# A new order of blocks and PSUM banks in a four-layer graph kernel

## What is computed

```python
x = _layernorm(x + _L0_gnn_ref(x, adj, ...))  # 8 heads: tanh(A * (Xc Xp^T)) Xp, relu
x = _layernorm(x + _L1_gnn_ref(x, adj, ...))  # two hypergraph convolutions, relu and norm between
x = _layernorm(x + _L2_gnn_ref(x, adj, ...))  # H = sum over k of (T^k X) Wk, T from exp(leaky_relu(sj + si)) * A
x = _layernorm(x + _L3_gnn_ref(x, adj, ...))  # gate, sigmoid(xg Wqk^T), scores * A, Wl and Wr
```

## Time and profile before

| | us |
|---|---|
| median of 3 runs | 1873.93 |
| lowest and highest run | 1869.39, 1875.06 |
| the profiled execution | 1869.13 |
| its span in the trace | 1867.3 |
| PE busy in the span | 1799.6 |
| DVE busy | 1657.4 |
| ACT busy | 1236.0 |
| POOL busy | 897.8 |

### The profile page before, as it was taken

How to read it: one execution, slowest core, us unless ns; L and a number is a source line. 1 busy time by engine, 2 the same in 40 slices (tenths; PEclk the granted TensorE clock), 3 DMA queues, 4 the chain that set the end, 5 groups by cost and what they waited for, 6 DMA issues and landing times. The chain is left out here.

```text
span 1867.3 us, 50617 instructions
## 1 busy us (share of the span) xinstructions
PE 1799.6 (96%) x14472; PEld 1569.0 (84%) x14472; DVE 1657.4 (89%) x4508; ACT 1236.0 (66%) x2384; POOL 897.8 (48%) x1743
## 2 busy tenths in 40 slices
PE   5789999999999999999999999999999999999985
PEld 4678888888888888888888888888888888888864
DVE  4779999999999999999999999999999999999874
ACT  4557666676676766766766766766667667676653
POOL 1335445445455455455545544544544545545542
PEclk9999999999999999999999999999999999999998
DMA  4111111211111111211111221111121111121110
GB/s 158 46 30 43 62 38 55 62 47 45 62 51 42 62 51 42 62 53 39 62 59 34 62 62 35 58 62 37 55 62 47 46 62 51 42 62 51 32 36 27
DMA packets 99483, 97.63 MB, mean 52 GB/s; under 512 B 8320, under 2 KB 90368, under 8 KB 99200
## 3 DMA queue, kind: packets, MB, share of 16 engines
q1 hardware_dynamic: 99456, 97.29, 17.0%
HBM read 80.48 MB, written 16.78 MB: 52 GB/s over the span
## 5 line engine op out<-in xcount | busy, mean ns | idle before, releaser
L416 ACT ACTIVATE x<-res,shift,rstd 128x256 f32<-128x256 f32 x512 | 283.4, 614 | 22.7 <-issue 10.4
L316 POOL TENSOR_TENSOR var_eps<-mean_var,eps 128x2 f32<-128x2 f32 x192 | 38.0, 198 | 417.2 <-DVE mean_var L618 417.2
L321 POOL TENSOR_TENSOR rstd<-var_eps,minus_half 128x2 f32<-128x2 f32 x256 | 194.3, 759 | 20.0
L626 DVE TENSOR_TENSOR masked<-psum,adjT 128x512 f32<-128x512 f32 x256 | 169.6, 684 | 23.0 <-PE psum L1035 23.0
L610 DVE BATCH_NORM_STATS2 stats<-res 128x6 f32<-128x256 f32 x512 | 189.5, 412 | 0.3
L969 PE MATMUL psum<-wk_hi,xT_hi 128*128 128x258 f32 (+1 forms) x512 | 186.2, 364 | 3.5 <-DVE res L920 2.1
L404 POOL TENSOR_TENSOR rz<-rz,vec 128x512 f32<-128x512 f32 x64 | 81.5, 1274 | 210.1 <-ACT rz L595 210.1
L969 PE MATMUL psum<-wk_hi,xT_lo 128*128 128x258 f32 (+1 forms) x512 | 173.6, 339 | 0.0
L969 PE MATMUL psum<-wk_lo,xT_hi 128*128 128x258 f32 (+1 forms) x512 | 173.5, 339 | 0.0
L969 PE MATMUL psum<-w_hi,zT_hi 128*128 128x256 f32 x512 | 147.0, 287 | 4.6 <-DVE zT_lo L605 4.6
L969 PE MATMUL psum<-w_hi,zT_lo 128*128 128x256 f32 x512 | 144.4, 282 | 0.0
(11 more groups left out here) (180 smaller groups left out, 6169.9 us busy)
## 6 DMA issues: line engine op xcount, KB each, us to landing
adjT<-in_adj_t SPq DMA_DIRECT2D x256, 128.0 KB, 2.3
xt_in<-in_xt SPq DMA_DIRECT2D x64, 256.0 KB, 2.7
x<-in_x SPq DMA_DIRECT2D x64, 256.0 KB, 2.8
out<-x SPq DMA_DIRECT2D x64, 256.0 KB, 2.2
wts<-in_adj SPq DMA_DIRECT2D x64, 128.0 KB, 2.2
wts<-in_w SPq DMA_DIRECT2D x1, 1028.0 KB, 10.6
wts<-in_w SPq DMA_DIRECT2D x1, 1024.0 KB, 7.3
wts<-in_w SPq DMA_DIRECT2D x1, 769.0 KB, 11.8
```

Source lines behind the costliest of these rows:

```text
L316: pool.tensor_tensor(var_eps[k][:, :], mean_var[k][:, :, 1], (eps_quarter if k == 1 else eps)[:, :], ALU.add)
L321: pool.tensor_tensor(rstd[k][:, :], var_eps[k][:, :], minus_half[:, :], ALU.pow) \
L416: last = act.activation(xs[k + 1][:, g, :], res[k][:, g, :], ACT.Identity, scale=rstd[k][:, g:g + 1], bias=shift[k][:, g:g + 1])
L626: dve.tensor_tensor(masked[:, q, :, :, :], ps(f"att_{q}").rearrange("p (g c n) -> p g c n", g=G, c=NC), adjT[0][:, :, :].unsqueeze(2).to_b ...
```

## The change

No computation is altered. The order of the blocks on all five engines, the banks of the PSUM tenants, and the places where weights are prepared in the first turns are new. Some blocks change the turn in which they run: the load of `xs[0]` and the tanh of heads 2 and 3 from stage 1 at the top to stage 0 at the bottom, `layer_stats(0)` and the reciprocal `att_r` from the bottom of a turn to the top of the next. PE's `claim` now takes several names and merges waits for one signal. The core of the diff:

```diff
 TENANTS = [
-    ("xp", 3, 0, "xp_read"), ("y12_0", 4, 4, "y12_read_0"), ("xpT", 6, 0, "xpT_read"), ("zT_0", 2, 2, "zT_lo_0"),
+    ("xp", 6, 0, "xp_read"), ("y12_0", 5, 4, "y12_read_0"), ("xpT", 4, 0, "xpT_read"), ("zT_0", 6, 2, "zT_lo_0"),
...
-    ("headsT", 1, 0, "headsT_read"), ("y0_0", 7, 3, "y0_read_0"), ("y0_1", 6, 3, "y0_read_1"),
-    ("mix_0", 2, 5, "mix_read_0"), ("heads", 4, 0, "res0"), ("mix_1", 1, 5, "mix_read_1"),
+    ("headsT", 5, 0, "headsT_read"), ("y0_0", 2, 3, "y0_read_0"), ("y0_1", 7, 3, "y0_read_1"),
+    ("mix_0", 0, 5, "mix_read_0"), ("heads", 4, 0, "res0"), ("mix_1", 1, 5, "mix_read_1"),
 ]
...
@@ POOL @@
+                if on[3]:
+                    rstd_of(1, n[3], p[3])
+                if on[6]:
+                    rstd_of(3, n[6], p[6])
                 if on[4]:
                     if t.first(4):
                         pool.wait_ge(sem("bk_bc"), 1)
                     wait(pool, "y0_read_1", n[4])
                     pool.tensor_tensor(y0[:, :, 0:D], y0[:, :, 0:D], rows(bk_bc), ALU.add).then_inc(sem("y0_bias"), 1)
-                if on[3]:
-                    rstd_of(1, n[3], p[3])
-                if on[6]:
-                    rstd_of(3, n[6], p[6])
+                if t.first(2):
+                    pool.wait_ge(sem("wlr_hi"), 1)
+                    pool.tensor_tensor(wlr_lo[:, :, :], wlr_f[:, :, :], value(wlr_hi[:, :, :]), ALU.subtract).then_inc(sem("wlr_lo"), 1)
+                    pool.wait_ge(sem("wk12_hi"), 1)
...
@@ ACT @@
-                if on[1]:
-                    wait(act, "pxT", p[1])
-                    wait(act, "x1_rest", p[1])
-                    normalise(0, n[1])
                 if on[0]:
                     wait(act, "att_3", p[0])
                     wait(act, "xcT", n[0])
                     act.activation(xcT[:, :, :, :].rearrange("p c g n -> p (c g n)"), ps("xcT"), ACT.Copy) \
                         .then_inc(sem("xcT_read"), 1)
...
+                if on[1]:
+                    wait(act, "pxT", p[1])
+                    wait(act, "x1_rest", p[1])
+                    normalise(0, n[1])
...
@@ DVE @@
+                if on[4]:
+                    wait(dve, "hop2_read", p[4])
+                    wait(dve, "hop1_1", n[4])
+                    sums, _ = both("hop1_0", "hop1_1", slice(D, D + 1))
+                    dve.tensor_scalar(row_s[:, :].unsqueeze(2), sums, 1e-12, None, ALU.add).then_inc(sem("rows_0"), 1)
+                if on[1]:
+                    wait(dve, "prop_read", n[1])
+                    dve.tensor_scalar(deg_m[:, :], prop[:, :, P], 1.2e-38, None, ALU.max).then_inc(sem("deg_inv_0"), 1)
+                if on[4]:
+                    wait(dve, "rows_0", n[4])
+                    dve.reciprocal(row_r[:, :], row_s[:, :]).then_inc(sem("rows_1"), 1)
...
@@ PE @@
-                    for q in range(NQ):
-                        claim(f"att_{q}", t)
+                    claim("att_0 att_1 att_2 att_3", t)
```

More of the change, by code:

```diff
@@ L434, in turn @@
                     hi(xT2_hi[:, :, :, :].rearrange("p c g n -> p (c g n)"), ps("xT2"), "xT2_hi")
[L435 to L439, removed]
+                if t.first(0):
+                    act.wait_ge(sem("w_0"), 32)
+                    act.activation(wp_hi[:, :, :], wp_f[:, :, :], ACT.Copy).then_inc(sem("wp_hi"), 1)
                 if on[0]:
@@ L445, in turn @@
                 if on[2]:
+                    wait(act, "z", p[2])
+                    wait(act, "hid_stats", p[2])
+                    wait(act, "hid_read_0", n[2])
+                    act.activation(hid_relu[:, 0, :], hid[:, 0, :], ACT.Relu).then_inc(sem("hid_relu_0"), 1)
                     wait(act, "z", p[2])
@@ L567, in turn @@
                     hi(pxT_hi[:, :, :, :].rearrange("p c g n -> p (c g n)"), ps("pxT"), "pxT_hi")
+                if on[0]:
+                    wait(act, "headsT", p[0])
+                    wait(act, "masked_1", n[0])
+                    act.activation(att[:, 0:2, :, :, :], masked[:, 0:2, :, :, :], ACT.Tanh).then_inc(sem("tanh_0"), 1)
                 if on[5]:
@@ L578, in turn @@
                     normalise(3, n[6])
[L579 to L582, removed]
+                if on[5]:
+                    wait(act, "mix_1", p[5])
+                    wait(act, "mix_read_1", p[5])
+                    wait(act, "rz_0", n[5])
+                    act.activation(rz3[:, 0, 0:2 * D], ps("rz_0"), ACT.Copy).then_inc(sem("rz_read_0"), 1)
                 if on[3]:
@@ L730, in turn @@
                     dve.tensor_tensor(bk_bc[:, :], bk_01[:, :], bk_3[:, 2, :], ALU.add).then_inc(sem("bk_bc"), 1)
-                if on[2]:
-                    if t.first(2):
-                        dve.wait_ge(sem("beta_w2"), 1)
-                    read_y1(0, n[2], p[2])
+                if on[4]:
+                    wait(dve, "hop2", p[4])
+                    wait(dve, "adj2_loaded", n[4], 16)
+                    wait(dve, "e_exp", n[4])
+                    dve.tensor_tensor(alpha[:, :, :], e_exp[:, :, :], adjT[2][:, :, :], ALU.mult) \
+                        .then_inc(sem("alpha"), 1)
+                if on[6]:
+                    layer_stats(3, n[6])
+                if t.first(2):
+                    dve.wait_ge(sem("wqk_hi"), 1)
+                    lo(wqk_lo[:, :, :], wqk_f[:, :, :], value(wqk_hi[:, :, :]), "wqk_lo")
+                if on[3]:
+                    aggregate(1, n[3], p[3])
+                if on[6]:
+                    aggregate(3, n[6], p[6])
                 if t.first(1):
@@ L828, in turn @@
                     last.then_inc(sem("hop2_read"), 1)
+                if t.first(1):
+                    dve.wait_ge(sem("beta_turned"), 1)
+                    dve.tensor_copy(beta_w2[:, :], ps("y1_0")[:, 0:D]).then_inc(sem("beta_w2"), 1)
+                if t.first(0):
+                    dve.wait_ge(sem("w_2"), 32)
+                    for a in range(2):
+                        for c in range(NC):
+                            dve.tensor_tensor(aw_prod[:, a * NC + c, :], wv_f[:, c, :], aw_bc[:, a, :], ALU.mult)
+                        last = dve.tensor_tensor(aw_prod[:, 2 * NC + a, :], bv_bc[:, :], aw_bc[:, a, :], ALU.mult)
+                    last.then_inc(sem("aw_prod"), 1)
+                    dve.wait_ge(sem("aw_prod"), 1)
+                    dve.tensor_reduce(u_col[:, :], aw_prod[:, :, :], AX.X, ALU.add).then_inc(sem("u_col"), 1)
                 if on[1]:
@@ L837, in turn @@
                 if on[0]:
-                    mask(3, n[0], p[0])
+                    wait(dve, "inc", n[0])
+                    dve.tensor_reduce(edge_n[:, :], inc[:, :, :], AX.X, ALU.add).then_inc(sem("edge_n"), 1)
                 if on[4]:
@@ L841, in turn @@
                 if on[0]:
-                    wait(dve, "inc", n[0])
-                    dve.tensor_reduce(edge_n[:, :], inc[:, :, :], AX.X, ALU.add).then_inc(sem("edge_n"), 1)
+                    wait(dve, "edge_n", n[0])
+                    dve.tensor_scalar(edge_m[:, :], edge_n[:, :], 1.0, None, ALU.max).then_inc(sem("edge_0"), 1)
+                if on[4]:
+                    aggregate(2, n[4], p[4])
+                if t.first(0):
+                    dve.wait_ge(sem("w1_hi"), 1)
+                    lo(w1_lo[:, :, :], w1_f[:, :, :], value(w1_hi[:, :, :]), "w1_lo")
                 if on[2]:
@@ L952, in claim @@
                 if not t.static:
-                    at = mates.index(u)
-                    mates = [mates[at - 1]]
+                    mates = [mates[mates.index(u) - 1]]
                 for v in mates:
                     _, _, stage, emptied = TENANTS[v]
-                    wait(pe, emptied, t.n[stage] if v < u else t.p[stage])
+                    yield emptied, t.n[stage] if v < u else t.p[stage]
+            def claim(names, t, *also):
+                found = {}
+                for signal, count in also:
+                    whole, part = part_of(signal)
+                    found[whole, count] = part or 0, signal
+                for name in names.split():
+                    if t.static and BANK[TENANT[name]] in taken:
+                        pe.wait_ge(sem("beta_w2"), 1)
+                    for signal, count in waits_of(name, t):
+                        whole, part = part_of(signal)
+                        found[whole, count] = max(found.get((whole, count), (0, "")), (part or 0, signal))
+                for (_, count), (_, signal) in found.items():
+                    wait(pe, signal, count)
             def claim_once(name, t):
@@ L1009, in y1_of @@
             def y1_of(g, t, n):
-                claim(f"y1_{g}", t)
-                wait(pe, f"zT_lo_{g}", n)
+                claim(f"y1_{g}", t, (f"zT_lo_{g}", n))
                 split_product(ps(f"y1_{g}")[:, 0:D],
@@ L1150, in turn @@
                     rz_of(0, t)
+                if t.first(1):
+                    pe.wait_ge(sem("beta_bc"), 1)
+                    claim_once("y1_0", t)
+                    for k in range(NK):
```

(10 more changed lines are left out.)

255 lines of the change are left out of this document (100 added, 155 removed), and 8 rows, old and new, of the table TENANTS.

## The result

The changed kernel is slower: 1881.48 us, the median of 7 runs (1878.35 to 1889.68), against 1873.93 us before (7 runs, 1869.39 to 1877.48). The ratio is 1.0048, with a 95% interval of 1.003 to 1.0066, so 0.5% and clear of no change. The forecast said 1894, slower by 1.1%.

The account below looks back on a forecast made before the run. PE, busy throughout the steady turns, was taken as the bound. From the profiled 1869.1 us, +26.6 (steady turns) and -3.4 (ramp and drain) gave 1892.3, or 1897.1 from the median; the forecast was 1894, range 1860 to 1905.

Parts of the forecast that it names:

- What bounds the kernel: Steady turns: PE busy throughout 27.76 us, so time freed on DVE or POOL buys nothing; only blocks reaching PE late count.
- deg_m inside y0_bias: Steady turn: deg_m, now before row_r, starts inside POOL's y0_bias and ends with it, 912.65 instead of 912.00, delaying hop1 reads.
- The walk: Following one steady turn's DVE and POOL instructions in the new order: hop2's weight load at 913.87 instead of 913.48.
- 59 x 0.45 = 26.6: Steady loss: PE waits 0.45 us more before hop2 in each of 59 turns, +26.6 us in all.
- I cost this at nothing: PE is busy throughout and hides it: Steady turns: edge_m, xg, e_exp and res3 leaving the port gain nothing, though edge_m alone gives DVE 0.5 us per turn.
- Ramp and drain: Outside the steady turns: waits for res0 and xcT saved, weight preparation and res3 costing; sum -3.4 us, from -6 to +3.
- the weight preparation: Ramp: wlr_lo and wk12_lo together on POOL in turn 2, in front of turn 3's xT0_lo; up to +2.3 us.
- xcT's wait: Ramp and drain: PE waits 4.2 us in three turns for xcT's read; the longest goes, -1.7 us.
- A: Rival, faster: deg_m starts before y0_bias or is spared the port, so hop2 is on time; 1860.4 us; chance 0.28.
- B: Rival, no difference: PE sees nothing of the change, ramp and drain exchange waits; 1869 to 1876 us; chance 0.14.
- C: Rival, slower: x_rest keeps xg off the port, PE's conv waits up to 1.0 us per turn; 1925 us; chance 0.03.
- D: Rival, slower: short POOL instructions also keep DVE out, rstd1's pow delaying inc through qkT 0.3 us; 1884 us; chance 0.03.

Follow-up runs that it names:

- y0_late: The changed kernel with an unused 0.69 us power instruction on POOL in front of y0_bias; 1854.79 us, 0.9886 of the kernel before.
- y0_plus: The changed kernel with an unused 0.20 us multiply on POOL in front of y0_bias; 1890.57 us, 1.0091 of the kernel before.
- deg_back: The changed kernel with only deg_m moved back behind the hop1 reads on DVE; 1855.35 us, 0.9894 of the kernel before.
- before_sj_edge: The kernel before with, on DVE, sj and sj5 in front of the first zT_lo and edge_m directly behind edge_n; 1880.73 us, ratio 1.0036.
- edge_back: deg_back with edge_m and edge_r moved behind deg on DVE, where edge_m stood in the kernel before; 1855.7 us, ratio 0.9902.
- ramp_free: The kernel before with POOL's x1_rest, in turns 2 to 5 only, waiting for the turn's second zT_lo; 1868.58 us, ratio 0.9978.
- best: deg_back with wlr_lo prepared in turn 3 on POOL and, in the drain, PE's xT2 before gram; 1852.49 us, ratio 0.9885.

## Why the prediction was right in place and wrong in size

**What bounds the kernel, right but for one conclusion.** The loss in the steady turns is PE's wait for one block, by tenths of a microsecond in each turn. That time freed on DVE buys nothing there did not follow; this is the step that failed, below.

**deg_m inside y0_bias, right.** The walk had y0_bias 0.40 us ahead of deg_m; it was 0.28. It had hop2's load 0.40 us later; 0.63 against 0.21 is 0.42. The missing 0.12 us of the lead arose mainly where the prediction had feared it: a small instruction of rstd1 met inc and took 0.33 us instead of 0.20, and y0_bias came later by about as much.

```profile
915.33 0.29 DVE L768 TENSOR_SCALAR inc<-adjT 128x256 f32<-128x256 f32 x1
...
915.34 0.33 POOL L315 TENSOR_TENSOR neg_mean<-mean_var,minus_one 128x2 f32<-128x2 f32 x1
```

The rule of the Trainium skill ("SBUF — State Buffer", section "SBUF: two separate sides", an exclusive lock kept by whoever starts first) agrees with y0_late and y0_plus for the long instructions. For a short POOL instruction that starts first it does not hold here: deg_m took 0.15 us inside the power instruction.

**The term of the sum that failed: 59 x 0.45 = 26.6.** Measured are 57 x 0.30 = 17.1 us (1599.57 and 1599.85 against 1582.45 and 1582.75). The wait at hop2 was nearly right, 0.42 us; I took 0.45 where the walk said 0.40. The step that failed is the sentence "I cost this at nothing: PE is busy throughout and hides it": other blocks of PE gave back 0.12 us per turn, of which three account for 0.08. PE's blocks, from the start of one to the start of the next (worked out from the start times in the traces, mean of 50 steady turns, us):

| PE's block | before | changed | deg_back | before_sj_edge |
|---|---|---|---|---|
| conv | 0.88 | 0.86 | 0.86 | 0.86 |
| qkT, hop2 | 2.27 | 2.69 | 2.18 | 2.27 |
| xT2, gram | 1.25 | 1.25 | 1.25 | 1.43 |
| z's transposes | 0.82 | 0.79 | 0.79 | 0.79 |
| y1 products | 2.91 | 2.87 | 2.87 | 2.88 |
| all others | 19.64 | 19.61 | 19.60 | 19.62 |

conv, z and y1 each wait 0.02 to 0.04 us before, together 0.08 per turn, too little for the list of waits. They vanish with the change, and all but 0.01 also in before_sj_edge. In the steady turn of that run only edge_m left the port, 0.17 us instead of 0.70; sj takes 0.2 us with or without the move. In edge_back edge_m stands in its old place, unstretched, and the turn stays at 27.56. So DVE's freed time was worth about 0.08 x 57 = 5 us; that it is the time and not the new places is likely, but no run takes the stretch alone away. PE's busy time, 27.76 of 27.76, does not show such gaps.

**Ramp and drain: the sum right by luck, its terms not.** I said -3.4. By PE's idle time the ramp gained 5.7 us and the drain lost 1.8, together -3.9. In the ramp, the weight preparation was right to the digit (the second wait for xT_lo, 10.8 less 8.5 us). xcT's wait fell from 4.2 us to 0.8, in two turns, where I had counted one and 1.7; but in the second trace of the kernel before it is only 2.5 us. The wait for res0, counted at -2.1, is gone. Not seen were 2.1 us of zT_lo, which ramp_free shows to be the port, in the very turns in which DVE is not covered. In the drain I had counted -1.9 for res3; instead xT2_lo waits 4.1 us there, 1.0 before. That gram stands in front of xT2 is a third of this, as best shows; the rest is open.

**What stays open.** Steady +17.1, ramp -5.7 and drain +1.8 make +13.2, and the mean spans of the two traces of each kernel differ by just that (1882.9 against 1869.75), since their busy times outside the steady part happen to be equal on the mean. But the medians differ by 7.6 (7 runs) and 6.9. Some 6 us are not accounted for. They lie between the traced executions and the medians: the two traced ones of the kernel before are 4.8 and 0.7 us below the medians of their runs, those of the changed kernel 8.2 above and 2.5 below, on the mean 2.7 below and 2.8 above. PE's busy time in the ramp differs by up to 7 us between two executions of one kernel; two traces each can't tell whether the kernel before loses more by this on the median. The figure of 1894 itself lay 3 us below what my sum gives from the median, 1897, and so came out closer than the sum did.

**The rivals.** A is the switch that y0_late threw, with a larger gain than I gave it (20 us instead of 8.7). B fell with the interval. C did not come: xg took 0.69 us in all turns. D fell with y0_late, as far as the power instruction goes.

## What to carry to other kernels

An instruction of 0.16 us that shares a port must be placed by the moment at which the other engine's long instruction starts, not by its own length; check each meeting from both engines' lists, and give it more than a few tenths of slack. A change of order that takes several meetings away and makes one new one is worth what the new one costs, if that stands in front of the bounding engine. Work freed under full cover may still be worth something: look at the starts of the bounding engine's blocks, not only at its busy share and its list of waits, and count ramp and drain apart, where nothing is covered.

## What the runs showed of the hardware

PE's speed in the ramp changes from execution to execution, and the column of the granted clock does not show all of it. xcT's four products of turn 1 in the two traces of the kernel before, first trace and then second:

```profile
32.07 1.13 PE L1085 MATMUL psum<-xpT,wts 128*128 128x256 f32 x4 [0.77 <-ACT xpT L507]
```

```profile
32.94 2.08 PE L1085 MATMUL psum<-xpT,wts 128*128 128x256 f32 x4 [0.77 <-ACT xpT L507]
```

From 33 to 45 us of the second trace the same products take nearly twice as long, as at the lower of the two clock levels (1.2 instead of 2.4 GHz), yet the window from 32.94 to 58.23 gives a mean clock of 1.00. The reason is that this trace has no record of the clock before 45.45 us (the first one, none before 30.38), and time without a record counts as full speed. At that moment PE's rows step from the long to the short duration:

```profile
45.06 0.58 PE L969 MATMUL psum<-w_lo,pxT_hi 128*128 128x512 f32 x1
45.48 0.39 PE L969 MATMUL psum<-w_hi,pxT_lo 128*128 128x512 f32 x1
```

This is where its ramp lost 5.5 us of busy time. With the time before the first record counted as the lower level, the two traces of the kernel before spend 30.4 and 45.5 us of the ramp there, those of the changed kernel 48.8 and 28.2, and PE's busy time in the ramp follows: 117.1 and 122.5, 123.0 and 115.7 us. Compare the durations of equal products, not only the column.

The stretch is handed on: in before_sj_edge two inc_b (128x128) took 2.00 us, the time of what was left of x_rest and y0_bias, as soon as sj no longer stood in front of them. An instruction that reads PSUM (row_s, 0.15 us at 918.23, inside y0_bias) is not held, and a 128x2 power instruction of 0.69 us on POOL held neither deg_m (y0_late) nor inc_b. The other way round, short POOL instructions are held: in the kernel before this one takes 0.64 us instead of 0.20, until 907.13, just behind the end of xg at 907.08. POOL's durations are rough in a profile, but the same happens in 59 turns.

```profile
906.49 0.64 POOL L316 TENSOR_TENSOR var_eps<-mean_var,eps_quarter 128x2 f32<-128x2 f32 x1
```
